# The last product of a feed-forward part as three products of rounded halves, in a one-core Trainium2 kernel

## The reference, cut to what matters

```python
x = x + h                              # h: the attention's output; D = 256
m = rms_norm(x)
y = jnp.square(jax.nn.relu(m @ W_fc)) @ W_proj      # W_fc: 256 x 1024, W_proj: 1024 x 256
return x + y
```

## Time and profile before

| | |
|---|---|
| median of 3 runs | 2468.99 us (2465.79 to 2471.11) |
| the profiled execution | 2469.22 us, its span 2467.5 us |
| granted TensorE clock, mean | 0.961 |
| TensorE busy in the span | 93% |
| VectorE busy | 73% |
| ScalarE busy | 44% |
| GpSimd busy | 31% |
| SBUF scratch for dynamic DMAs | the default |

### The profile page before, as it was taken

One profiled execution on the slowest core, in us unless ns is written; L12 is line 12 of the kernel. 1 busy time (PEld: TensorE's weight loads), 2 busy tenths in 40 slices (PEclk: granted clock), 3 DMA queues, 4 the chain that ended last, 5 costly groups with the idle time before them and its releaser, 6 DMA issues.

```text
span 2467.5 us, 50870 instructions
## 1 busy us (share of the span) xinstructions
PE 2302.4 (93%) x15131; PEld 2066.0 (84%) x15131; DVE 1810.9 (73%) x4353; ACT 1086.8 (44%) x2287; POOL 760.3 (31%) x1562
## 2 busy tenths in 40 slices
PE   4589999999999999999999999877599999999998
PEld 4468988888889889888898888755599999999887
DVE  6577887888878878878888877377667677667553
ACT  2334343444443443433444443355555455555442
POOL 0113333332332332333323323100233344434332
PEclk9699999999999999999999999865899999999999
DMA  5322212212212122122122121589544545554340
GB/s 189 102 34 46 44 35 46 42 36 49 40 36 51 37 44 47 35 46 42 35 48 41 36 50 27 170 292 304 200 160 145 178 149 172 166 159 162 133 128 18
DMA packets 369736, 232.85 MB, mean 94 GB/s; under 512 B 261612, under 2 KB 343920, under 8 KB 360464
## 3 DMA queue, kind: packets, MB, share of 16 engines
q1 hardware_dynamic: 317136, 200.35, 28.2%
q0 software_dynamic: 11280, 29.31, 4.2%
q10 hardware_dynamic: 41264, 2.51, 1.1%
HBM read 176.19 MB, written 57.67 MB: 95 GB/s over the span
## 4 chain that ended last, share of the span: by engine, by line
PE 85%; DVE 7%; DMA 2%; ACT 2%; issue 2%; SPq 2%; POOL 0%; DVEq 0%; ACTq 0%; POOLq 0%
PE ps_front L780 13%; PE ps_back L2038 11%; PE ps_inva L780 9%; PE ps_invb L780 9%; PE ps_back L780 8%; PE ps_back L2099 5%; PE ps_back L2082 5%; PE ps_front L1984 5%; PE ps_back L2107 5%; PE ps_inva L2004 2%; PE ps_invb L2021 2%; PE ps_front L1977 2%; PE ps_invb L2023 1%; PE ps_inva L2006 1%; PE ps_inva L414 1%
## 5 line engine op out<-in xcount | busy, mean ns | idle before, releaser
L643 DVE TENSOR_TENSOR w_lo<-w_raw,w_hi 128x512 fp32r<-128x512 f32 x288 | 190.0, 688 | 3.9
L780 PE MATMUL ps_back<-w_hi,eh_hi 128*128 128x256 f32 x624 | 180.1, 289 | 3.2 <-DVE eh_lo L653 3.2
L780 PE MATMUL ps_back<-w_hi,eh_lo 128*128 128x256 f32 x624 | 176.4, 283 | 0.0
L780 PE MATMUL ps_back<-w_lo,eh_hi 128*128 128x256 f32 x624 | 176.4, 283 | 0.0
L732 ACT ACTIVATE w_hi<-w_raw 128x512 fp32r<-128x512 f32 x288 | 169.5, 626 | 0.0
L744 ACT ACTIVATE sact<-ps_inva 128x512 f32<-128x512 f32 (+1 forms) x96 | 49.8, 519 | 236.1 <-PE ps_inva L780 236.1
L1367 ACT ACTIVATE v_s<-ps_front 128x512 f32<-128x512 f32 x64 | 38.1, 595 | 247.5 <-PE ps_front L780 247.5
L1367 ACT ACTIVATE g_s<-ps_front 128x512 f32<-128x512 f32 x64 | 38.3, 598 | 239.9 <-PE ps_front L780 229.5
L1272 POOL TENSOR_SCALAR xrow_v<-bag 128x1 f32<-128x1 f32 x31 | 6.8, 220 | 428.9 <-DVE bag L1821 428.9
L780 PE MATMUL ps_inva<-xT_hi,w_hi 128*128 128x512 f32 (+1 forms) x384 | 135.2, 352 | 1.7 <-DVE xT_lo L648 1.7
L2038 PE MATMUL ps_back<-state,kqT_t 128*128 128x128 f32 x1024 | 133.1, 283 | 3.8 <-DVE r_s L1742 2.5
(11 more groups left out here) (391 smaller groups left out, 6871.2 us busy)
## 6 DMA issues: line engine op xcount, KB each, us to landing
w_raw<-wts_d SPq DMA_DIRECT2D x72, 1024.0 KB, 5.2
wts_d<-prep SPq DMA_DIRECT2D x96, 256.0 KB, 3.8
dT<-alphaT_d SPq DMA_DIRECT2D x32, 512.0 KB, 3.7
prep<-L_ffn_W_gate_dram SPq DMA_DIRECT2D x32, 256.0 KB, 3.3
prep<-L_ffn_W_up_dram SPq DMA_DIRECT2D x32, 256.0 KB, 3.7
prep<-L_ffn_W_down_dram SPq DMA_DIRECT2D x32, 256.0 KB, 4.3
x_all<-L_attn_x_dram SPq DMA_DIRECT2D x4, 1024.0 KB, 10.0
hTr<-hT_d SPq DMA_DIRECT2D x32, 128.0 KB, 3.8
```

Of the source, the lines that this page charges most:

```text
L643: V.tensor_tensor(piece(w_lo[p], m).bitcast(F32R), piece(w_raw, m), piece(w_hi[p], m), ALU.subtract).then_inc(split[n], 1)
L780: ins = MM(out_, w[a].bitcast(F32R), x[b].bitcast(F32R), start=start and n == 0, stop=stop and n == 2)
```

## The change

`W_proj` is split once, before the loop: ScalarE rounds it into the new tile `wproj_hi`, VectorE makes `wproj_lo`, which lies on the bytes of `wproj`. In each tile ScalarE makes the Relu, then the square of it (into `hid_sq`, the bytes of `o_s`), then the rounded copy `hid_hi` (the bytes of `hid`), each behind a wait for the one before; VectorE, in place of the product, makes `hid_lo` as a difference, also on the bytes of `o_s`. TensorE makes 24 fp32r products in place of 8 float32 ones. To make room in SBUF for `wproj_hi`, the scratch for dynamic DMAs (those that GpSimd issues) is set to 8192.

```diff
+        with nc.sbuf_tensor("tails_ahead", [P, 2 * KD * HD], F32), nc.sbuf_tensor("wproj_lo", [P, FB, D], F32) as wproj_lo:
+            pass
         tails = at("tails", [P, 3 * KD * HD])
...
+        wproj_hi = at("wproj_hi", [P, FB, D])
...
-        hid = oT
+        hid, hid_sq = oT, o_s
...
             def tail_fc(t):                                   # ScalarE
                 for n in range(2):
-                    evac(t + 1, BU_FC + n, hid[:, n * GW:(n + 1) * GW], ACT.Relu)
+                    u, s = BU_FC + n, slice(n * GW, (n + 1) * GW)
+                    evac(t + 1, u, hid[:, s], ACT.Relu)
+                    act.wait_ge(back_evac[u % 2], b_evac(t + 1, u))
+                    A(hid_sq[:, s], hid[:, s], ACT.Square).then_inc(hid_squared, 1)
+                    act.wait_ge(hid_squared, 4 * t + 2 * n + 1)
+                    A(hid_hi[:, s].bitcast(F32R), hid_sq[:, s], ACT.Copy).then_inc(hid_squared, 1)
...
                 silu(0, n, True)
+            act.wait_ge(tail_loaded, 16 * (3 + KD))
+            A(wproj_hi[:, :, :].bitcast(F32R), wproj, ACT.Copy).then_inc(vg_hi_ready, 1)
             blocks_y(0)
...
             def tail_fc(t):                                   # VectorE
                 for n in range(2):
-                    u = BU_FC + n
-                    dve.wait_ge(back_evac[u % 2], b_evac(t + 1, u))
+                    dve.wait_ge(hid_squared, 4 * t + 2 * n + 2)
                     s = slice(n * GW, (n + 1) * GW)
-                    V.tensor_tensor(hid[:, s], hid[:, s], hid[:, s], ALU.mult).then_inc(hid_ready, 1)
+                    V.tensor_tensor(hid_lo[:, s].bitcast(F32R), hid_sq[:, s], hid_hi[:, s], ALU.subtract).then_inc(hid_ready, 1)
...
             decay_products(1)
+            dve.wait_ge(vg_hi_ready, 4 * KD + 1)
+            V.tensor_tensor(wproj_lo[:, :, :].bitcast(F32R), wproj, wproj_hi[:, :, :], ALU.subtract).then_inc(vg_split, 1)
             pair_products(0), pair_inverse(0)
...
                     if fb % (FB // 2) == 0:                   # TensorE, tail_proj
                         pe.wait_ge(hid_ready, 2 * t + fb // (FB // 2) + 1)
-                    last = MM(ps[:, 0:D], hid[:, fb * P:(fb + 1) * P], wproj[:, fb, :], start=fb == 0, stop=fb == FB - 1)
+                    b = slice(fb * P, (fb + 1) * P)
+                    for n, (h, w) in enumerate(((hid_hi, wproj_hi[:, fb, :]), (hid_hi, wproj_lo[:, fb, :]), (hid_lo, wproj_hi[:, fb, :]))):
+                        last = MM(ps[:, 0:D], h[:, b].bitcast(F32R), w.bitcast(F32R), start=fb == 0 and n == 0, stop=fb == FB - 1 and n == 2)
...
             pe.wait_ge(tail_loaded, 16 * (3 + KD))
+            pe.wait_ge(vg_split, 4 * KD + 1)
...
-    nc = _bacc.Bacc("TRN2", target_bir_lowering=False, num_devices=1)
+    nc = _bacc.Bacc("TRN2", target_bir_lowering=False, num_devices=1, dynamic_dma_scratch_size=8192)
```

More of the change, by code:

```diff
@@ L205, in program @@
         k_s = at("k_s", [P, 2, HD])
-        xi, yi, state, r_s, u_s, qsg, o_s, oT, gw = (at(n, [P, HD]) for n in ("xi", "yi", "state", "r_s", "u_s", "qsg", "o_s", "oT", "gw"))
+        xi, yi, state, r_s, u_s, qsg = (at(n, [P, HD]) for n in ("xi", "yi", "state", "r_s", "u_s", "qsg"))
+        with nc.sbuf_tensor("hid_lo", [P, HD], F32) as hid_lo:
+            pass
+        o_s = at("o_s", [P, HD])
+        with nc.sbuf_tensor("hid_hi", [P, HD], F32) as hid_hi:
+            pass
+        oT = at("oT", [P, HD])
+        gw = at("gw", [P, HD])
         ti = at("ti", [P, HD // 2])
@@ L350, in program @@
         sk_dve, sk_act, sk_pe = sem("sinkhorn_dve"), sem("sinkhorn_act"), sem("sinkhorn_pe")
-        rt_dve, rt_pe, pi_ready = sem("routing_dve"), sem("routing_pe"), sem("pi_ready")
+        rt_dve, rt_pe, hid_squared = sem("routing_dve"), sem("routing_pe"), sem("hid_squared")
         te_ready = sem("te_ready")
@@ L717, in act_late @@
             act.wait_ge(sk_dve, SK_D * (ROUNDS // GROUP))
-            A(pi, la[:, :, :], ACT.Exp).then_inc(pi_ready, 1)
-            act.wait_ge(pi_ready, 1)
+            A(pi, la[:, :, :], ACT.Exp).then_inc(sk_act, 1)
+            act.wait_ge(sk_act, SK_A * (ROUNDS // GROUP) + 1)
             with nc.allow_non_contiguous_dma(reason="weights beside each row"):
```

## The result

The changed kernel takes 2477.35 us (median of 7 runs, 2473.74 to 2478.99), the kernel before beside it 2470.39 (7 runs, 2465.79 to 2471.12). The ratio is 1.0035, 95% interval 1.0025 to 1.0044: slower by more than the 0.2% that can be told from no change. The forecast was 2457 us, with a chance of 0.12 for slower. The profiled execution took 2473.74 us, its span 2471.9.

A forecast was written before the change was run, and what follows sets the result against it. TensorE held 85% of the chain, with an equally long VectorE road, so both must shorten. 12.9 + 0.95 - 0.9 = 13.0 us off 2469.22 gave 2456.2 profiled, 2456.0 for runs; small losses made it 2457, range 2450 to 2469.

The forecast's parts named there:

- No wait, with 0.5 us in hand: Start of tail_proj: VectorE's hid_ready at 748.98 and 750.78, ahead of TensorE's need at 749.78 and 751.3.
- TensorE's product length: tail_proj in each tile: 24 fp32r products take 2.95 us against 3.49 before, 0.54 us shorter.
- ScalarE's gaps: Semaphore gap between dependent Relu, square and copy on ScalarE: taken as 0.03 us, bounded by 0.03 and 0.20.
- the third and second rival: ScalarE's gaps in each tile: at 0.1 us, 2465 (second, chance 0.18); with 0.20, 2478 (third, chance 0.12).
- VectorE's list: Differences and scans ahead of the residual sum x1: x1 starts 6.68 us behind the first Relu, mean gain 0.445 us.
- Two roads, a tile gains what both gain: From tail_proj to the row transpose: TensorE's list and VectorE's from x1 equally long within some 0.1 us; both must shorten.
- The last tail: Final tail, standing alone: 12 products after the second hid_ready end at 1607.7 against 1606.79, 0.9 us later.
- W_proj's split: Before the loop: ScalarE's copy 2.1 us and VectorE's difference 2.7 us fall into idle time, costing nothing; 5 us if uncovered.
- The scratch: GpSimd's dynamic DMAs in the experts' stage: halved scratch taken to cost 0, bounded by 5 us.
- The sum: Whole kernel: 29 tails x 0.445 = 12.9 us, plus 0.95, less 0.9, net 13.0 us faster.
- The rival that ended slower: Road over ScalarE and VectorE becomes the longer bound: with gaps of 0.20, 9 us slower, 2478; chance 0.12.
- The rule on relu and multiply: Squares in each tile: the skill page's VectorE layout would be 0.06 us per tile slower, 2 us in all.

The follow-up runs named there:

- the two extra copies: Changed kernel plus two 128x256 ScalarE copies to idle row buffers, between the second rounded copy and the copies to u_s; 2497.28 us, ratio 1.0116.
- e1_own_bank: Changed kernel with tail_proj accumulating in a bank idle at that time instead of the shared back bank; 2449.39 us, ratio 0.9936 to the kernel before.
- e4_scratch_alone: Kernel before the change with only the scratch of the dynamic DMAs set to 8192; 2467.01 us, ratio 1.0004.
- e2_products_alone: Kernel before with 24 fp32r products, ScalarE's and VectorE's lists kept, high half replacing the low one (timing only); 2446.96 us, ratio 0.9925.
- f2_early_copy: Changed kernel with the first copy to u_s moved ahead of ScalarE's second rounded copy, bank still shared; 2461.92 us, ratio 0.9977.

## Why the prediction was wrong

**The step that failed** is the sentence "`copy_u` ends at 751.1 in place of 749.98 + 0.60 = 750.58 and isn't needed before 752.7". The new end of `copy_u` was worked out nearly right. (It measured 4.69 us behind the first Relu, the forecast's 751.1 is 4.75.) But I asked only who reads `u_s`, which is `state_p`, and not who waits for the bank that the copy empties. Its first half frees the bank of `tail_proj`, and by the forecast's own numbers that was 750.06 + 0.53 = 750.6, 0.8 us behind the start at 749.78 that I left unmoved. The row that would have told it is in ScalarE's timeline of before:

```profile
749.03 0.60 ACT L1434 ACTIVATE u_s<-ps_back 128x512 f32<-128x512 f32 x1 [0.30 <-PE ps_back L2038]
```

The copy's first half ended at 749.63, 0.15 ahead of the product. After, it ends at some 751.93 + 0.58 = 752.5, and the product starts at 752.64, again some 0.14 behind; with the two extra copies at 759.46 + 0.57 = 760.03 and 760.16, 0.13. `copy_u` had next to no slack before the change; the wait only didn't show, since TensorE was busy with `state_u` until then (in `e1_own_bank`, where no bank is waited for, the product starts 3.37 us behind the Relu, 0.06 earlier than before the change). So "No wait, with 0.5 us in hand" was right of the operand (in `e1_own_bank` the product never waits for it) and wrong of the product.

**TensorE's product length**: right, 2.95 forecast, 2.93 to 2.97 measured in the loop. The 2.62 worked out from a formula for one matmul doesn't hold for a row of 24.

**ScalarE's gaps**: right. The square starts 748.92 - 748.90 = 0.02 behind the Relu's end and the copy 0.04 behind the square's; 0.03 was taken, and the third and second rival, which hung on gaps of 0.1 and 0.14, fall.

**VectorE's list**: right, but hidden. `e1_own_bank` shows it as the limit at 6.62 for the 6.68 forecast, at a gain of 45.35 - 44.81 = 0.54 us a tile for the 0.445 forecast.

**Two roads, a tile gains what both gain**: the road over x1 is right. In every kernel (four inner tiles of each) the transpose of the normalised row starts 8.98 to 9.02 us behind x1 and 0.13 behind the end of VectorE's row, as before the change. TensorE's own list is as long within 0.1 us: in `e1_own_bank`, with x1 late by VectorE's list, TensorE stands idle for 753.53 - 753.46 = 0.07 us ahead of the transpose.

```profile
753.07 0.39 PE L790 MATMUL ps_front<-wqk_hi,hT_lo 128*128 128x512 f32 x1
...
753.53 0.43 PE L2135 MATMUL ps_back<-ident,rows 128*128 128x128 f32 x2
```

In the kernels whose x1 waits for TensorE this idle time is 0.02 us at most, so both roads end together, and no run makes TensorE's list the later one, so that half of the rule isn't shown. What I hadn't drawn lies ahead of both roads: bank, copy, ScalarE.

**The last tail**: right, +0.9 forecast. Its x1 starts 1612.47 - 1606.15 = 6.32 us behind its first Relu, before it was 1607.07 - 1601.75 = 5.32, so 1.0 later. There `state_u` is absent, and the product waits for the difference, not for a bank.

**W_proj's split**: hidden, as forecast. ScalarE's copy at 111.84 takes 1.91 us and lies ahead of an idle stretch of 12.26 us (13.97 before); VectorE still sits idle for 2.69 of its 5.25 us ahead of 126.61.

```profile
111.84 1.91 ACT L1546 ACTIVATE wproj_hi<-tails 128x2048 fp32r<-128x2048 f32 x1
...
126.00 1.08 ACT L1377 ACTIVATE k_s<-ps_front 128x512 f32<-128x512 f32 x2 [12.26 <-issue]
```

**The scratch**: right, `e4_scratch_alone`.

**The sum**: with the missing wait the tile changes by +0.91 - 0.60 = +0.31, not by -0.445; 29 tiles make +9, with the last tail +10, against 7.0 between the medians. The other 3 aren't explained; the step from the 30th to the 31st, shorter by 1.5 to 3.1 us in the profiles of the changed kernel, is the place where the traces show such a difference. The rival that ended slower named the right engine and the wrong mechanism: longer gaps, where it was the list's plain length ahead of a copy that frees a bank. Its 2478 is near the measured time by accident.

**The rule on relu and multiply**: two squares and two rounding copies are what lengthens the list ahead of the copy, so the squares are half of it. The Trainium skill's page "ScalarE: Activation LUTs", section "Rules for kernel authors", would have them on VectorE. I priced that at 0.06 us per tile against the rule, by duration, and the trace after has the same durations, 0.63 for a square on ScalarE. What the list ahead of the copy costs was not in that price. `e2_products_alone`, with the squares on VectorE (and no low half), is the one kernel with fp32r products, the shared bank and ScalarE's old order, and its product doesn't wait for the copy. It doesn't separate the rule from the missing low half; the rule's own layout wasn't run.

## What to carry to other kernels

When a list on one engine grows, write down for every instruction behind it not only who reads what it writes but who waits for what it *empties*: the next use of the bank or buffer it frees. Where a start in the trace lies just behind the end of a copy on another engine, take it for a dependence until the code rules it out. And an evacuation that frees a shared bank goes ahead of work that nobody waits for yet: moving one such copy by one place was worth 1.0035 - 0.9977 = 0.6% here, a bank of its own 1.0%.

## What the runs showed that I had not expected

- ScalarE's instructions in a row start 0.53 us apart at 128x512 when they don't wait for each other (749.59 to 750.12 after), and 0.66 when they do (750.73 to 751.39). An independent instruction put between two dependent ones costs less than its length: in `f2_early_copy` the square, the copy to `u_s` and the rounding start at 747.81, 748.35 and 748.82, so that the square and the rounding stand 1.01 us apart in place of 0.66, for a copy of 0.58.
- A kernel's period repeats within 0.02 us between executions, while the time up to the first x1 differs by 1 to 2 us and a single step at the stage's end by 1.6. A change of 0.3 us in a tile is read from the period, not from the span.
- The chain's share of an engine says little of what a microsecond on another is worth: ScalarE was busy 44% of the span before and 47% after and had 6% of the chain after, and 0.62 us more on it made each tile 0.60 longer.
